# The last product-key layer stores its own rows, and both product-key layers gate in one instruction

## The reference, cut to what matters

```python
def _rmsnorm(x, w, eps=1e-06):
    inv = jax.lax.rsqrt(jnp.mean(x * x, axis=-1, keepdims=True) + eps)
    return x * inv * w
...
H, DK, K = (8, 128, 8)       # heads, key width, experts kept per head
NKEYS = 32
NEXP = NKEYS * NKEYS         # 1024 experts, expert_down and expert_up are [1024, 128]
```

## Time and profile before

| | |
|---|---|
| time, median of three runs | 2700.26 us (2692.53 to 2700.63) |
| span of the profiled execution | 2696.5 us |
| time of the profiled execution outside its span | not shown; the median of the runs is 3.8 us above the span |
| busy over the span | PE 78%, DVE 84%, ACT 69%, POOL 60% |
| `k5a`: first `hid` to last | 1650.3 to 2096.3 us |
| `k7a`: first `hid` to last | 2236.9 to 2682.8 us |
| `hid`, L2116 | 64 instructions in each of the two stages |
| statistics in both stages, L2128 | 56 in the loops and 8 in the peeled parts |
| last DMA, L3021 | 1 of 2048 KB, issued at 2687.43 us |

### The profile page before, as it was taken

How to read it: one execution, slowest core, us unless ns; L and a number is a source line. 1 busy time by engine, 2 the same in 40 slices (tenths; PEclk the granted TensorE clock), 3 DMA queues, 4 the chain that set the end, 5 groups by cost and what they waited for, 6 DMA issues and landing times. The chain is left out here.

```text
span 2696.5 us, 59529 instructions
## 1 busy us (share of the span) xinstructions
PE 2097.3 (78%) x17450; PEld 1738.0 (64%) x17451; DVE 2266.7 (84%) x5645; ACT 1862.5 (69%) x4275; POOL 1615.9 (60%) x1472
## 2 busy tenths in 40 slices
PE   4748888879599999693488877888888448888887
PEld 2336666658488888573466656777777227777776
DVE  6489999875688888657888867999999779999997
ACT  3579999756455555563255548989988349898896
POOL 0069999727200000374566538999999119999996
PEclk9869999989899999896799989999999669999999
DMA  2013333241200000111100000000000000000001
GB/s 60 3 47 97 96 98 95 71 144 52 62 1 0 0 0 1 53 52 35 40 2 0 0 1 1 0 0 0 0 0 0 0 1 1 0 0 0 0 0 32
DMA packets 67736, 70.66 MB, mean 26 GB/s; under 512 B 10264, under 2 KB 46320, under 8 KB 67504
## 3 DMA queue, kind: packets, MB, share of 16 engines
q1 hardware_dynamic: 61488, 57.56, 7.3%
q0 software_dynamic: 4992, 10.23, 1.4%
q10 hardware_dynamic: 1120, 1.22, 0.2%
HBM read 57.32 MB, written 11.67 MB: 26 GB/s over the span
## 5 line engine op out<-in xcount | busy, mean ns | idle before, releaser
L1899 POOL TENSOR_TENSOR k7a_psums<-k7a_sims 128x1024 f32<-128x1024 f32 x224 | 421.4, 1913 | 19.0 <-DVE k7a_w L2107 14.1
L1899 POOL TENSOR_TENSOR k5a_psums<-k5a_sims 128x1024 f32<-128x1024 f32 x224 | 421.3, 1912 | 18.4 <-DVE k5a_w L2107 14.1
L994 POOL TENSOR_TENSOR mc_hc<-mc_h,mc_cs 128x512 f32<-128x512 f32 x256 | 327.5, 1294 | 33.1 <-DVE mc_h L961 17.3
L1964 PE MATMUL k5a_pw<-g_ident,k5a_w 128*128 128x128 f32 x2048 | 265.5, 277 | 72.3 <-DVE k5a_hid L2116 47.9
L1964 PE MATMUL k7a_pw<-g_ident,k7a_w 128*128 128x128 f32 x2048 | 265.5, 277 | 72.1 <-DVE k7a_hid L2116 47.9
L1964 PEld LDWEIGHTS k5a_pw<-g_ident,k5a_w 128*128 128x128 f32 x2048 | 226.8, 141 | 115.6 <-DVE k5a_w L2107 52.7
L1964 PEld LDWEIGHTS k7a_pw<-g_ident,k7a_w 128*128 128x128 f32 x2048 | 226.8, 141 | 115.4 <-DVE k7a_w L2107 52.4
L961 DVE TENSOR_TENSOR_SCAN mc_h<-mc_dA,mc_inj 128x512 f32<-128x512 f32 x256 | 298.6, 1200 | 2.3 <-PE mc_inj L850 1.8
L2107 DVE SCALAR_TENSOR_TENSOR k7a_w<-k7a_psums,k7a_best,k7a_lift 128x1024 f32<-128x1024 f32 x224 | 279.4, 1272 | 0.5 <-ACT k7a_lift L2035 0.3
L2107 DVE SCALAR_TENSOR_TENSOR k5a_w<-k5a_psums,k5a_best,k5a_lift 128x1024 f32<-128x1024 f32 x224 | 279.4, 1272 | 0.5 <-ACT k5a_lift L2035 0.3
L2035 ACT ACTIVATE k5a_lift<-k5a_psums 128x1024 f32<-128x1024 f32 x224 | 228.4, 1020 | 35.3 <-DVE k5a_w L2107 30.9
(11 more groups left out here) (515 smaller groups left out, 5881.9 us busy)
## 6 DMA issues: line engine op xcount, KB each, us to landing
mc_cs<-c_rows SPq DMA_DIRECT2D x128, 256.0 KB, 3.1
e_w<-in_L_ffn_W_dram SPq DMA_DIRECT2D x16, 256.0 KB, 5.7
token_rows<-e_zn SPq DMA_DIRECT2D x16, 256.0 KB, 3.9
e_zn<-token_out SPq DMA_DIRECT2D x16, 256.0 KB, 4.9
g_X<-in_L_attn_a_x_dram SPq DMA_DIRECT2D x8, 256.0 KB, 5.8
out_dram<-g_X SPq DMA_DIRECT2D x1, 2048.0 KB, 8.7
e_zs<-token_rows,e_token POOLq DMA_INDIRECT x78, 2.6
token_out<-e_ys,e_token POOLq DMA_INDIRECT x78, 2.3
```

The costliest lines, as they stand in the source:

```text
L994: nc.gpsimd.tensor_tensor(hc[:, q % RH, :], h_[:, q % RB, :], cs[:, S % RC, :], ALU.mult).then_inc(outs, 1)
L1899: nc.gpsimd.tensor_tensor(psums[:, h - 1, :, :], rows_of(p, h), s2, ALU.add).then_inc(pooled, 1)
L1964: ins = nc.tensor.matmul(pw[:, j, :], w[:, h % WR, j * P:(j + 1) * P], env.ident[:, :], start=(h == 0 and j % 4 == 0), stop=(h == HD - 1 a ...
```

## The change

The last product-key layer is handed the output tensor. In it no statistics are taken, and a list for SP is added: it waits for `added` to reach 4, 8, ..., 28, 30, 31 and 32, and stores the tiles that are done since the last value, ten DMAs in all, then waits for all of them. DVE waits at its end for `added` in place of `measured`. The function `store` goes. In both product-key layers `hid` is written by one instruction of 128 x 1024.

```diff
--- before.py
+++ after.py
@@ -1846,7 +1846,7 @@
     return env.product_keys, weights
 
 
-def product_keys(nc, env, raw, tag):
+def product_keys(nc, env, raw, tag, out=None):
 
 
 
@@ -1874,7 +1874,7 @@
             lift = ps("lift", [P, LR, NE])
             pw, phd, pmix = ps("pw", [P, J, P]), ps("phd", [P, J // 2, P]), ps("pmix", [P, 512])
             SHARE, GROUPS = K // 2, 4
-            floored, asummed = sem("floored"), sem("asummed")
+            floored, asummed, stored = sem("floored"), sem("asummed"), sem("stored")
             copied, scored, s_in, pooled, dsummed, topped, crossed, ranked, lifted, weighed, summed, hidden, gelud, \
                 mixed, made, added, measured = (sem(x) for x in (
                     "copied", "scored", "sin", "pooled", "dsummed", "topped", "crossed", "ranked", "lifted", "weighed",
@@ -2112,10 +2112,7 @@
                     need(dve, gelud, 2 * t + 2)
                     need(dve, made, t)
                     need(dve, summed, (t + 1) * HD)
-                    for q in range(2):
-                        ins = nc.vector.tensor_tensor(hid[:, 4 * q:4 * q + 4, :], gl[:, p, 4 * q:4 * q + 4, :],
-                                                      pw[:, 4 * q:4 * q + 4, :], ALU.mult)
-                    ins.then_inc(mixed, 1)
+                    nc.vector.tensor_tensor(hid[:, :, :], gl[:, p, :, :], pw[:, :, :], ALU.mult).then_inc(mixed, 1)
 
                 def residual(t):
 
@@ -2152,15 +2149,30 @@
                         weigh(t, p, 5)
                         if not begun:
                             residual(t - 1)
-                            statistics(t - 1)
+                            if out is None:
+                                statistics(t - 1)
                         weigh(t, p, 6)
                         weigh(t, p, 7)
 
                 rounds(dve, NT // 2, body)
                 finish(NT - 1, 1)
                 residual(NT - 1)
-                statistics(NT - 1)
-                dve.wait_ge(measured, NT)
+                if out is None:
+                    statistics(NT - 1)
+                    dve.wait_ge(measured, NT)
+                else:
+                    dve.wait_ge(added, NT)
+
+            @block.sync
+            def _(sp):
+                if out is not None:
+                    rows = out.rearrange("b (s p) c -> p (b s) c", p=P)
+                    ends = [*range(TPC, NT, TPC), NT - 2, NT - 1, NT]
+                    for t0, t1 in zip([0] + ends[:-1], ends):
+
+                        sp.wait_ge(added, t1)
+                        sp.dma_start(rows[:, t0:t1, :], env.X[:, t0:t1, :]).then_inc(stored, 16)
+                    sp.wait_ge(stored, 16 * len(ends))
 
 
 def rotary_weights(nc, ctx, a, tag):
@@ -3011,18 +3023,6 @@
                 residual(GH - 1)
 
 
-def store(nc, env, out):
-    with ExitStack() as ctx:
-        stored = ctx.enter_context(nc.semaphore("stored"))
-        block = ctx.enter_context(nc.Block())
-
-        @block.sync
-        def _(sp):
-            sp.dma_start(out.rearrange("b (s p) c -> p (b s) c", p=P), env.X[:, :, :]).then_inc(stored, 16)
-
-            sp.wait_ge(stored, 16)
-
-
 STAGES = ("mamba", "experts", "attention", "experts", "rotary", "product_keys", "state_space", "product_keys")
 
 
@@ -3077,7 +3077,7 @@
             if s == "state_space":
                 state_space(nc, env, env.raw["state_space"], f"s{i}")
             if s == "product_keys":
-                product_keys(nc, env, env.raw["product_keys"], f"k{i}")
+                product_keys(nc, env, env.raw["product_keys"], f"k{i}", out if i + 1 == len(stages) else None)
             if s == "experts":
                 loads = []
                 if env.expert_weights is None:
@@ -3091,7 +3091,6 @@
             if s == "mamba":
                 mamba(nc, env, of("L0_attn_a_"))
             sweep(nc)
-        store(nc, env, out)
 
 
 def shape_constants():
```

## The result

The kernel after takes 2682.41 us (median), the kernel before 2700.45 in the runs beside it: a ratio of 0.9939, with a 95% interval of 0.9925 to 0.9953. That is faster, by 0.6%; 2684.5 was forecast. One of the four runs of the kernel after fell into a slower state (2796.21 us, mean granted clock 0.811 and not 0.935); the ratio leaves it out, and so it is not the quotient of the two medians. The profiled execution of the kernel after took 2683.22 us, 1.7 more than its span of 2681.5.

The account below looks back on a forecast made before the run. The bound was taken to be a loop through DVE's head and then packed PE. Statistics 3.1 + 0.8, gating 4.3 and store 7.6 summed to 15.8 us: span 2680.7, time 2684.5 us, range 2674 to 2692.

Parts of the forecast that it names:

- The bound: Product-key loop: `hid`, `w` 1, top-8, `w` 2 on DVE, then 9.1 us of packed PE; neither engine alone bounds it.
- Statistics: `k7a`: DVE wins 0.49 us a tile, the loop 0.11; 3.1 us over 28 tiles, plus 0.8 in the last two.
- The first tile with its 14.35: First tile of `k7a`, where `w` 7 comes in time: taken as the period with `w` 7 off the loop.
- Gating: `hid` as one instruction in both product-key layers: 0.067 us less a tile, 4.3 us over 64 tiles.
- Rival D: `hid` in both layers: the second half's whole start-up of 0.16 us goes, 10.2 us for 4.3; span 2678.6; chance 0.04.
- Store: End of the kernel: 10.5 us behind the last residual fall to 2.9, a gain of 7.6 us.
- The estimate of 2.15 us: Last 64 KB store: its length if about 2.0 us are fixed for each DMA; the prediction took 1.7 instead.
- The sum: Whole kernel: 15.8 us less, span 2680.7 us, time 2684.5 us (-0.59%).
- A: `k7a` loop: DVE is the bound, its whole 0.49 us a tile arrives, 10.6 us more gain; span 2673.9; chance 0.10.
- B: Product-key loops: neither loop edit arrives, gain only 8.4 us; span 2691.9; chance 0.15.
- C: End of the kernel: last piece and both ends cost as much as the old store, gain 8.2 us; chance 0.05.
- E: Product-key stage: TensorE granted its lower clock, 7.2 us more a tile; kernel slower, 2713; chance 0.04.

Follow-up runs that it names:

- the dose of DVE work: Kernel after with one, then three idle `bn_stats` a tile behind the residual in the last layer; `k7a` period 14.28 us with one, 14.48 with three.
- the moved top-8: Kernel after with top-8 behind `w` 2, `k5a` statistics behind `w` 7, POOL's head 2 sums before the candidates; 2666.7 us, ratio to before 0.9884.
- The store alone: Kernel before with only the store changed, ten groups from inside the last stage, statistics still taken; ratio to before 0.9975.
- the four-instruction kernel: Kernel after with `hid` written by four 128x256 instructions in both layers; periods 14.59 us in `k5a`, 14.48 in `k7a`.
- reordering: Kernel after with `k5a` statistics behind `w` 7, top-8 behind `w` 2 and behind DVE's half of head 0's sums; 2657.62 us, ratio to before 0.9858.
- gating alone: Kernel before with only `hid` written by one instruction in both layers; ratio to before 0.9978, period 14.40 us in both.
- statistics alone: Kernel before with only the last layer's statistics left out, store still behind the stage; ratio to before 0.9982, `k7a` period 14.35 us.

## Why the prediction was right

*The bound.* Right. Chain, then one tile on DVE and on PE, gave a loop through both engines; the dose of DVE work (nothing, then 0.20) and the moved top-8 (0.17 to 0.22 less) show both halves of it. The gap ahead of `hid`, counted as in the prediction from the start of `w` 0, went from 0.19 to 0.53 (2407.25 - 2405.54 - 1.185); about 0.5 was forecast.

*Statistics.* 0.51 a tile on DVE (0.70 to 0.19 from residual to `w` 6) for 0.49, and 0.11 on the loop as forecast: 14.46 to 14.35 alone. The first tile with its 14.35 was the right witness. The last two tiles won 0.37 and 0.39, forecast 0.39 each.

*Gating.* 1.285 to 1.221 on the instruction and 14.46 to 14.40 on the loop, 0.06 for 0.067, in both layers. Rival D, and with it the reading of the Trainium skill's fixed term (VectorE: DVE Perf Modes, section on the TRN2 errata) as time at the issue, fails: four instructions cost 0.063 more each, not 0.16.

*Store.* 8.0 for 7.6. The wait on SP is 0.03 and not 0.1, the landing 1.54 and not 1.7, the two ends 1.00 and not 1.07: all small, all to one side. The store alone showed 2.72 for the landing, so a single execution can be 1.2 us off. The estimate of 2.15 us from the Trainium skill's figures (DMA: Bandwidth & Descriptors, section on the anatomy of one DMA; they are for DMAs issued by POOL) is above fifteen of the sixteen landings of 64 KB and below the late one; here the measured 1.54 decides.

*The sum.* 15.9 from the three touched stretches, 15.8 forecast; the rest of the span moved by 0.9 the other way. The time came out 2.1 below the forecast, and one reason is the 3.8 us that I took as lying outside the span: in 39 runs of the kernel before with both on record, the time is 1.85 to 2.28 above the span, so the rest of the 3.8 was a profiled execution faster than the median one. In the kernel after it is 1.7. That the time fits to 2 us is therefore partly luck; the stretches above, and not the time, bear the prediction out.

*Rivals.* A and B are out by the periods of the parts, C by the 2.57 us. E did not happen in the kernel after. Its mechanism does exist in this loop, as the four-instruction kernel shows, but its price was wrong: a middle tile with such a stretch cost 15.21 - 14.59 = 0.62 or 15.21 - 14.48 = 0.73 us, not 7.2, because the clock was back within the tile and part of the slow stretch ran in time that PE would have waited anyway.

## What to carry to other kernels

When two engines alternate in a loop, taking work from one of them is worth only what it takes off the path that crosses between them: find the instruction of each that the other waits for, and ask of every other one only whether it makes that one late. A peeled first iteration with slightly other timing is a free experiment on that. And work that can't be removed can be moved behind such an instruction: reordering won another 0.8% (ratio to before from 0.9939 to 0.9858, some 22 us), where leaving the statistics out had won 4 us.

## What was not expected

Code that no kernel here touches differs between profiles by more than a part of this change. The rotary stage's first matmuls to its attention (`r4p` to `r4a`) took 75.4 us before and 75.6 after, but 70.6 in the kernels with gating alone and statistics alone, and 73.8 in that with the store alone. Its granted clock differs; the same 60 us of that stage before and with gating alone (PE busy first, PEclk third from the end):

```profile
1247.00:1307.00 60.00, 37.53 (x160) 32.35 (x160) 55.51 (x133) 19.86 (x60) 37.13 (x43) 0.73 0.00 1
```
```profile
1247.00:1307.00 60.00, 32.84 (x160) 28.60 (x160) 59.01 (x147) 21.78 (x67) 41.09 (x48) 0.78 0.00 1
```

The stage spreads over 5 us, the runs of the kernel before over twice that, from 2692.5 to 2703.1. Whether that stage is what spreads them I did not measure; it is why single parts are judged here by periods inside the two stages and not by spans.

The other surprise is the clock with `hid` in four instructions. PE's wait ahead of a tile's first transposes is 1.59 to 1.69 us there, in every tile of both stages, and ten stretches at 0.50 fall into `k5a` and five into `k7a`. In the eleven other profiles that wait is 1.39 to 1.56, and neither stage holds such a stretch. The longer wait goes with the falls, then, in one execution of one kernel; that it causes them is argued and not shown, and what picks the tiles stays open.
